# The order of the first expert product, and a final layer norm moved partly into the last unit

## What is computed

```python
x = layernorm(x + attention(x, w_qkv))
gate = softmax(x @ Wg + bg); weights = top2 of gate, normalised
h = gelu(einsum('bsd,edf->bsef', x, W1) + b1)
y = einsum('bsef,efd->bsed', h, W2) + b2
x = layernorm(x + einsum('bsed,bse->bsd', y, weights))
```

## Time and profile before

| what | value |
|---|---|
| median of 3 runs | 4650.12 us (4573.87 to 4879.95) |
| the profiled execution | 4573.87 us |
| its span, first to last instruction, slowest core | 4572.2 us |
| spans of all cores | 4561.7 to 4572.2 us |
| start of the first product of phase y, first unit | 956.6 us |
| last vector accumulation of the last unit | starts at 4488.07 us |

### The profile page before, as it was taken

How to read it: one execution, slowest core, us unless ns; L and a number is a source line. 1 busy time by engine, 2 the same in 40 slices (tenths; PEclk the granted TensorE clock), 3 DMA queues, 4 the chain that set the end, 5 groups by cost and what they waited for, 6 DMA issues and landing times.

```text
span 4572.2 us, 48275 instructions; the slowest of 8 cores (4561.7 to 4572.2 us)
## 1 busy us (share of the span) xinstructions
PE 4088.5 (89%) x19431; PEld 1914.3 (42%) x19776; DVE 1141.7 (25%) x1978; ACT 903.0 (20%) x1415; POOL 76.6 (2%) x92
## 2 busy tenths in 40 slices
PE   5865555599999999999999999999999999999993
PEld 3333333244444444444444444444444444444442
DVE  1116767511111111111111111111111111111115
ACT  1224444211111111111111111111111111111112
POOL 0000000000000000000000000000000000000000
PEclk9975555599999999999999999999999999999996
DMA  6551000022222222222222222222222222222211
GB/s 112 103 96 36 19 19 19 1 37 37 37 37 37 37 37 37 37 37 37 37 37 37 37 37 37 37 37 38 41 41 41 41 40 37 37 37 37 37 19 74
DMA packets 97483, 187.26 MB, mean 41 GB/s; under 512 B 3426, under 2 KB 24290, under 8 KB 97258
## 3 DMA queue, kind: packets, MB, share of 16 engines
q0 software_dynamic: 89616, 157.36, 19.7%
q1 hardware_dynamic: 7650, 26.81, 1.6%
HBM read 333.12 MB, written 8.39 MB: 75 GB/s over the span
## 4 chain that ended last, share of the span: by engine, by line
PE 85%; DVE 6%; issue 3%; DMA 2%; ACT 2%; DVEq 1%; ACTq 0%; POOLq 0%; SPq 0%
PE ps_y L151 39%; PE ps_h L151 39%; PE ps_qk L151 4%; PE ps_sc L151 2%; PE ps_pt L151 2%; DMA W1g<-wqkv 1%; DVE stats L401 1%; ACT probs_u L409 1%; ACT hpr L812 1%; DVEq L157 1%; DVE attn_sb L479 1%; DMA W2g<-wqkv 0%; DVE outb L913 0%; DVE xpre L494 0%; DVE probsT L437 0%
## 5 line engine op out<-in xcount | busy, mean ns | idle before, releaser
L151 PE MATMUL ps_y<-W2g,hpr 128*128 128x512 bf16 x8029 | 1764.5, 379 | 55.5 <-ACT hpr L812 47.0
L151 PE MATMUL ps_h<-x1T,W1g 128*128 128x512 bf16 x8027 | 1765.9, 379 | 9.0 <-issue 0.3
L835 DVE SCALAR_TENSOR_TENSOR y_acc<-ps_y,wgt,y_acc 128x1024 f32<-128x1024 f32 x512 | 657.4, 1284 | 2932.4 <-PE ps_y L151 2932.4
L151 PEld LDWEIGHTS ps_y<-W2g,hpr 128*128 128x128 bf16 x8192 | 799.3, 98 | 1020.8 <-issue 61.6
L151 PEld LDWEIGHTS ps_h<-x1T,W1g 128*128 128x128 bf16 x8192 | 801.9, 98 | 968.5 <-issue 3.3
L812 ACT ACTIVATE hpr<-ps_h,b1T 128x1024 bf16<-128x1024 f32 x512 | 570.5, 1114 | 2957.1 <-PE ps_h L151 2957.1
L151 PE MATMUL ps_sc<-k_b,q_b 64*128 64x384 bf16 x256 | 122.6, 480 | 205.0 <-ACT probs_u L409 203.2
L409 ACT ACTIVATE probs_u<-ps_sc,stats 128x384 bf16<-128x384 f32 x256 | 149.3, 583 | 231.5 <-DVE stats L469 224.6
L151 PE MATMUL ps_qk<-xT_S,W1g 128*128 128x512 bf16 (+3 forms) x629 | 137.4, 386 | 43.3 <-DMA W1g<-wqkv 35.0
L401 DVE TENSOR_REDUCE stats<-ps_sc 128x1 f32<-128x384 f32 x256 | 139.8, 550 | 8.8 <-issue 2.7
L151 PE MATMUL ps_pt<-I_b,probs_u 128*128 128x128 bf16 x768 | 128.4, 305 | 1.2 <-ACT probs_u L409 1.2
(11 more groups left out here) (89 smaller groups left out, 680.1 us busy)
## 6 DMA issues: line engine op xcount, KB each, us to landing
W1g<-w POOLq DMA_DIRECT2D x32, 2048.0 KB, 13.7
W2g<-w POOLq DMA_DIRECT2D x32, 2048.0 KB, 13.2
W1g<-wqkv POOLq DMA_DIRECT2D x20, 1024.0 KB, 9.4
xch_q<-xh SPq DMA_DIRECT2D x18, 512.0 KB
xch<-xh SPq DMA_DIRECT2D x16, 512.0 KB
out<-outb SPq DMA_DIRECT2D x16, 512.0 KB, 2.6
W2g<-wqkv POOLq DMA_DIRECT2D x1, 2048.0 KB, 21.6
mask_s<-maskl SPq DMA_DIRECT2D x1, 192.0 KB
```

The lines of the kernel that those rows point to most:

```text
L151: lambda t: t.matmul(_d, _l, _r, start=_s, stop=_e))(dst, lhsT, rhs, start, stop)
L835: ev = DV((lambda _tq, _pp, _e: lambda v: v.scalar_tensor_tensor(out=y_acc[:, _tq, :], in0=ps_y[_pp][:], scalar=wgt[:, _tq, _e:_e + 1], in ...
```

## The change

Two things are changed, both from the 32 units on.

First, in phase h the two outer loops change places: all 8 blocks `fc` of the first half of the tokens come first, then all 8 of the second half. Chunks 0 to 7 of phase y now wait for the last Gelu of the first half (`gel_pr[0]`), chunks 8 to 15 for that of the second (`gel_pr[1]`).

```diff
-        for fc in range(8):
-            for pr in range(2):
-                bank = bk_h[(fc * 2 + pr) % 2]
+        for pr in range(2):
+            for fc in range(8):
+                bank = bk_h[(pr * 8 + fc) % 2]
...
-                    w_ = [(s_w2, wld["w2", u]), (s_ac, gel_last)]
+                    w_ = [(s_w2, wld["w2", u]), (s_ac, gel_pr[tq // 8])]
```

```diff
+    fpair = {i: (0 if i <= 8 else (1 if (i - 9) % 2 == 0 else 0)) for i in range(NCH)}
...
     def plan_trans_fin(i):
-        s = i % 2
+        s = fpair[i]
+        pv = prevu.get(s)
...
             if dc == 0:
-                w_ = tbank[s].rw() + [(s_dv, y_done)]
-                if (i - 2) in sqf_v:
-                    w_.append((s_ac, sqf_v[i - 2]))
+                w_ = tbank[s].rw()
+                if pv in sqf_v:
+                    w_.append((s_ac, sqf_v[pv]))
...
-        w_ = [(s_mm, tbk), (s_dv, y_done)] + fbank[s].rw()
...
+        w_ = [(s_mm, tbk), (s_dv, yev31[i])] + fbank[s].rw()
...
+            if u == NUNIT - 1:
+                yev31[tq] = ev
+                if tq <= 8:
+                    if tq >= 1:
+                        plan_fintail(tq - 1)
+                    plan_trans_fin(tq)
...
-    for i in range(NCH):
+    for i in range(9, NCH):
         plan_trans_fin(i)
-        if i >= 1:
-            plan_fintail(i - 1)
+        plan_fintail(i - 1)
     plan_fintail(NCH - 1)
```

More of the change, by code:

```diff
@@ L844, in build_nc @@
-    y_done = p.val[s_dv]
-    if debug:
-        for i in range(NCH):
[L847 to L850, removed]
     tbank = [bk_h[0], bk_y[0]]
@@ L854, in build_nc @@
     fin_v, sqf_v, ap_v, st_v, tbk_v = {}, {}, {}, {}, {}
+    fpair = {i: (0 if i <= 8 else (1 if (i - 9) % 2 == 0 else 0)) for i in range(NCH)}
+    prevu = {}
     def plan_trans_fin(i):
-        s = i % 2
+        s = fpair[i]
+        pv = prevu.get(s)
         tbk = None
@@ L870, in plan_trans_fin @@
         tbk_v[i] = tbk
-        w_ = [(s_mm, tbk), (s_dv, y_done)] + fbank[s].rw()
[L872 to L875, removed]
+        w_ = [(s_mm, tbk), (s_dv, yev31[i])] + fbank[s].rw()
+        if pv in ap_v:
+            w_.append((s_dv, ap_v[pv]))
+        if pv in sqf_v:
+            w_.append((s_ac, sqf_v[pv]))
         fin_v[i] = DV((lambda _i, _s: lambda v: v.scalar_tensor_tensor(
@@ L882, in plan_fintail @@
     def plan_fintail(j):
-        s = j % 2
+        s = fpair[j]
         sqf_v[j] = AC((lambda _s, _p: lambda sc_: sc_.activation(
@@ L920, in plan_fintail @@
                      waits=[(s_dv, ap_v[j])], inc=s_st)
-    for i in range(NCH):
+        prevu[s] = j
+    yev31 = {}
+    for u in range(NUNIT):
+        e, qf = u // 4, u % 4
+        gel_pr = {}
+        hend = None
+        for pr in range(2):
+            for fc in range(8):
+                bank = bk_h[(pr * 8 + fc) % 2]
+                gend = None
+                for tt in range(2):
+                    tq5 = pr * 2 + tt
+                    for dc in range(8):
+                        w_ = [(s_w, wld["w1", u])]
+                        if tt == 0 and dc == 0:
+                            w_ += bank.rw()
+                        gend = MM(bank.ap[:, 512 * tt:512 * (tt + 1)],
+                                  W1g[:, dc, 128 * fc:128 * (fc + 1)],
+                                  x1T[:, dc, 512 * tq5:512 * (tq5 + 1)],
+                                  start=(dc == 0), stop=(dc == 7), waits=w_,
+                                  inc=(s_mm if (tt == 1 and dc == 7) else None))
+                hend = gend
+                col = 8 * (qf * 8 + fc) + e
+                gel_pr[pr] = AC((lambda _fc, _pr, _bk, _col: lambda s: s.activation(
+                    out=hpr[:, _fc, 1024 * _pr:1024 * (_pr + 1)], in_=_bk.ap[:],
+                    func=AF.Gelu, bias=b1T[:, _col:_col + 1]))(fc, pr, bank, col),
+                    waits=[(s_mm, gend)], inc=s_ac)
+                bank.release = [(s_ac, gel_pr[pr])]
+        wld["w1", u + 1] = GP((lambda _u: lambda e_: e_.dma_start(out=W1g[:], in_=w1_ap(_u)))(u + 1),
+                              waits=[(s_mm, hend)], inc=s_w) if u + 1 < NUNIT else None
+        yend = None
+        for tq in range(NCH):
+            pp = tq % 2
+            bank = bk_y[pp]
+            gend = None
+            for dh in range(2):
+                for fc in range(8):
+                    w_ = [(s_w2, wld["w2", u]), (s_ac, gel_pr[tq // 8])]
+                    if dh == 0 and fc == 0:
+                        w_ += bank.rw()
+                    gend = MM(bank.ap[:, 512 * dh:512 * (dh + 1)],
+                              hpr[:, fc, 128 * tq:128 * (tq + 1)],
+                              W2g[:, fc, 512 * dh:512 * (dh + 1)],
+                              start=(fc == 0), stop=(fc == 7), waits=w_,
+                              inc=(s_mm if (dh == 1 and fc == 7) else None))
+            yend = gend
+            ev = DV((lambda _tq, _pp, _e: lambda v: v.scalar_tensor_tensor(
+                out=y_acc[:, _tq, :], in0=ps_y[_pp][:], scalar=wgt[:, _tq, _e:_e + 1],
+                in1=y_acc[:, _tq, :], op0=ALU.mult, op1=ALU.add))(tq, pp, e),
+                waits=[(s_mm, gend)], inc=s_dv)
+            bk_y[pp].release = [(s_dv, ev)]
+            if u == NUNIT - 1:
[4 more added lines that the diff above has]
+                    plan_trans_fin(tq)
+        if u + 1 < NUNIT:
+            wld["w2", u + 1] = GP((lambda _u: lambda e_: e_.dma_start(out=W2g[:], in_=w2_ap(_u)))(u + 1),
+                                  waits=[(s_mm, yend)], inc=s_w2)
@@ L923, in build_nc @@
+    y_done = p.val[s_dv]
+    if debug:
+        for i in range(NCH):
+            SY((lambda _i: lambda e: e.dma_start(out=d_y[128 * _i:128 * (_i + 1), :], in_=y_acc[:, _i, :]))(i),
+               waits=[(s_dv, y_done)], inc=s_x)
+            SY((lambda _i: lambda e: e.dma_start(out=d_w[128 * _i:128 * (_i + 1), :], in_=wgt[:, _i, :]))(i),
+               inc=s_x)
+    for i in range(9, NCH):
         plan_trans_fin(i)
-        if i >= 1:
-            plan_fintail(i - 1)
+        plan_fintail(i - 1)
```

## The result

The changed kernel is faster by 1.4%: the ratio of its times to those of the kernel before is 0.9857, with a 95% interval of 0.9841 to 0.9874. Its profiled execution took 4513.62 us; the lowest of its times is 4508.86 and their median 4513.43. The kernel before, run again beside it, had its lowest times at 4573.87, 4577.68 and 4577.76. Forecast were 4506 us and a gain of 68; the two profiled executions are 60.3 apart, and the medians of the undisturbed ones (4577.68 and 4510.65) 67.0. Executions of every kernel here are at times disturbed, with TensorE's clock at 0.81 in stretches of the units on one die or both (67.2 us for 256 products instead of 55.2, in one that was profiled), and these readings leave them out.

The account below looks back on a forecast made before the run. TensorE was taken to bound the units, a chain through VectorE and ScalarE the last 83 us. Removing the Gelu waits (52 us) and moving nine final chunks (16 us) takes 68 from 4573.87: 4506 us, range 4490 to 4592.

Parts of the forecast that it names:

- the base: Whole kernel: 68 us taken from the profiled execution's 4573.87, giving 4506; from the median of 4650.12, 4582.
- rival B: In the units: without the 1.6 us rest TensorE loses its clock, slower than before, 4582 us; chance 0.15.
- Part 1: Phase h's order in the 32 units: TensorE's wait for the last Gelu goes, 1.63 us a unit, 52 us.
- The lower bound from the idle records: In the units: TensorE's 32 recorded waits for the last Gelu sum to 47.0 us, the least gain.
- Part 2: Nine final chunks moved inside the last phase y: 16 us saved, with 6 and 19.5 as ends.
- the 110 to 114: Sign at the kernel's end: last fin about 110 to 114 us after Y, the start of the last phase y.
- The step of 6.26: Final chunks inside the last phase y: VectorE's chain sets 6.26 us a chunk if the clock never falls.
- The sum: Whole kernel: 52 + 16 = 68 us from the profiled 4573.87 gives 4506; ends 4521 and 4502.
- A: Final chunks inside the last phase y: clock stays low, steps of 7.9 us, 6 us saved there, 4516; chance 0.17.
- C: Final chunks inside the last phase y: steps 2.4 us above 6.26, so nothing saved there, 4522; chance 0.08.
- The current limit: In the units: a rule of 13/16 clock would add about 800 us; the trace, at 1.00, was said to disagree.

Follow-up runs that it names:

- the part 2 kernel: Changed kernel with phase h's loops and the wait for the last Gelu as before, nine final chunks inside the last phase y; 4563.14 and 4569.69 us.
- part 1 alone: Kernel before with only phase h by halves and the split wait for the Gelus; 4526.88, 4533.4 and 4592.14 us, ratio 0.985.
- the interleaved kernel: Changed kernel with the last unit's second half of phase h spread over phase y's chunks 0 to 7, all 16 final chunks inside; 4483.72 us, ratio 0.9789.

## Why the prediction was right, and where not

*The step that failed: the base.* The mechanism and its size in like executions came out. What failed is where the 68 us were taken from. The prediction set its sum on one execution, 4573.87, and left the two other times shown, 76 and 306 us above it, as an excess that "nothing in its instructions explains". It let the excess ride on: the same gain from the median was put at 4582, and rival B and the range up to 4592 got their price from it. The runs show in its place that the excess is not part of what the change acts on. The kernel before has it in 8 of 11 executions and the changed one in 3 of 9 (4628.56, 4885.12 and 4921.1 us, with the mean clock of at least one die at 0.84 to 0.90 instead of 0.92); the others lie at 4573.87 to 4577.76 and at 4508.86 to 4513.62. Set against the median of 4650.12 that stands in the table of the kernel before, 4506 is a fall of 144 us, 3.1%, and more than twice what came, 65 to 67 us and 1.4%. Against like executions it is 68. A median of three times that lie 306 us apart is no base for a forecast.

*Part 1, 52 us.* Right to a tenth: 110.5 us a unit was worked out from starts, and 110.51 came. The lower bound from the idle records, 47, was 5 short; the part 2 kernel, which keeps the rests, still shows 46.8 of them beside its 112.13. Nothing took the wait's place, and the loads stayed hidden (`W1g` took 17.4 us to landing in this profile and 13.8 in the second one of the same kernel).

*Part 2, 16 us.* 14.7 came, with the last fin at Y+115.2, outside the 110 to 114 that were to show it right. Fin 1 was put at Y+15.1 and ended at Y+15.1. The step of 6.26 was 6.39 at full clock; 0.4 on top was taken for the clock and 6.66 came. That the sum 6.66 was hit is partly luck: of the 0.40 above 6.26, 0.13 is the step itself, 0.05 the single pause, and about 0.23 the clock (the first step, at 6.32, gives 0.01 back). That TensorE would slow down, fill its step and so get its clock back was in the text; that this makes it alternate step by step was not. The term that was mis-sized is the one behind fin 8: I ran chunks 9 to 15 at the full clock, and chunk 9 began at the low one, 1.7 us (24.40 us from fin 8 to fin 9, and 22.73 with the clock kept up).

*The sum.* 66.7 against 68. The other 6.4 us of the distance between 4506 and the profiled 4513.6 are a term that the sum put at nothing: the stretch ahead of the first phase y, which lost its one rest of 1.6 us and still ended 4.8 later on the slowest core. I compared with one execution and gave its front part no spread of its own, beyond the 0.3%.

*The rivals.* A fell: its step of 7.9 needed a clock that stays low, and the windows show 0.74 and 1.00 by turns. B fell: part 1 alone runs at 1.00 in the units, 110.5 us each from the first to the last. Its 4582 was a wrong price as well, since the excess of 76 us that it used is in the kernel before too. C fell, 8.7 a step against 6.66.

*The current limit.* I wrote that the trace disagrees with the rule of the Trainium skill ("TensorE: Matmul & The Clock Gate", section "Seeing it yourself"), 13/16 of the clock for a die with three cores in dense products. With eight dense cores at 1.00 that stands for the executions compared here. But 13/16 is 0.8125, and the section on the result names units at 0.81. So the rule gives that lower clock rightly, but not that it holds whenever three cores are dense, and why it is seen in some executions only stays open.

## What to carry to other kernels

A wait for the last of many steps can often become a wait for the last step that the next work truly reads, once the producer is ordered by what the consumer reads first; the order alone gains nothing, and the gain is read from start to start, not from idle records. When a serial tail goes beside dense work, its length per chunk is the pace, so shorten that chain (here a bank less in it and other work in its hops, tried together) before anything else. An engine that then rests between bursts can lose its clock and pay at the next dense stretch too; work that fills the rest, even work that nobody reads, can then be worth its place. And a gain is forecast from an execution like those it will be compared with: look for the times that repeat, not at the median of a few that lie far apart.

## What was not expected of the hardware

The clock alternates with the load: where the final chunks stand behind phase h and nothing fills the rests, a rest of 2.71 to 4.40 us was followed by a slow chunk (0.74 over the step in the changed kernel), and one of 0.44 to 0.92 by a fast one, with 9 chunks and with 16, to the last step. In the interleaved kernel rests of 2.33 and one of 2.53 us were followed by fast chunks, and those of 2.68, 2.71 and 2.79 by slow ones (their 16 products took 4.74, 4.61 and 4.97). And extra products, 8 for each of eight chunks, made the kernel 3.3 us shorter from the start of the last phase y.
